# First layer's small heads: parts in half of the array's rows, groups in alternating halves, scores and turned scores issued in turn

## What is computed

```python
xn = _layernorm(x, axis=-1)
q, k, v = split(xn @ qkv_w + qkv_b)          # 16 heads of 8 features
a = softmax(q @ k.T * scale, axis=-1) @ v    # per head, no mask in this layer
x = x + (a @ proj_w + proj_b) + moe(xn)
```

## Time and profile before

| | |
|---|---|
| median of three runs | 2050.64 us (2049.12 to 2058.69) |
| the profiled execution | 2065.7 us, of which 2063.9 us from first to last instruction |
| mean granted clock of PE in it | 0.95 |
| first layer's heads in it | from 102.5 us; last new head's scores at 340.9 us |
| PE busy over the span | 1846.2 us (89%) |
| DVE, ACT, POOL busy | 1512.0 (73%), 973.7 (47%), 900.6 (44%) us |

### The profile page before, as it was taken

The page is one execution under the profiler, slowest core; times in us unless marked ns, Lnnn a source line. Parts: engine busy times, 40 slices in busy tenths (PEclk is TensorE's granted clock), DMA queues, the critical chain, the costliest instruction groups (busy, mean ns, idle before and its releaser), DMA issues. The chain is left out here.

```text
span 2063.9 us, 33097 instructions
## 1 busy us (share of the span) xinstructions
PE 1846.2 (89%) x9971; PEld 1013.2 (49%) x9971; DVE 1512.0 (73%) x4413; ACT 973.7 (47%) x2251; POOL 900.6 (44%) x1307
## 2 busy tenths in 40 slices
PE   6399998578998994899799999989999999999998
PEld 3233333345555662334466666744445555555543
DVE  6477776476664765899577677657877787888898
ACT  3167676246664442622377777733333333333332
POOL 1566661045552330112066677745544455433341
PEclk9789999579999995999899999999999999999999
DMA  8552222363232006990465446411131443524211
GB/s 283 140 117 36 29 29 51 49 245 81 38 75 39 23 22 123 159 196 24 120 195 154 147 142 185 132 50 45 44 107 56 127 119 88 137 71 109 61 32 31
DMA packets 240309, 201.81 MB, mean 98 GB/s; under 512 B 26853, under 2 KB 222731, under 8 KB 239498
## 3 DMA queue, kind: packets, MB, share of 16 engines
q1 hardware_dynamic: 222042, 171.29, 33.1%
q0 software_dynamic: 17376, 28.29, 5.5%
q10 hardware_dynamic: 720, 0.11, 0.0%
HBM read 116.74 MB, written 82.89 MB: 97 GB/s over the span
## 5 line engine op out<-in xcount | busy, mean ns | idle before, releaser
L2845 DVE SCALAR_TENSOR_TENSOR x<-f_m,f_gs,x 128x128 f32<-128x128 f32 x1024 | 353.4, 348 | 81.7 <-PE f_m L2670 54.7
L512 DVE TENSOR_REDUCE a_nmax<-a_s 128x1 f32<-128x512 f32 (+3 forms) x512 | 278.9, 585 | 125.6 <-PE a_s L323 51.9
L2218 POOL TENSOR_SCALAR a_lg<-a_lg,a_rinv 128x256 f32<-128x256 f32 (+1 forms) x256 | 226.4, 902 | 150.4 <-DVE a_rinv L2255 149.9
L2670 PE MATMUL f_m<-f_wo,f_oT 128*128 128x512 f32 x512 | 261.4, 595 | 1.7 <-DVE x L2845 1.0
L428 ACT ACTIVATE a_pT<-a_st 128x512 f32<-128x512 f32 (+3 forms) x512 | 228.8, 519 | 35.1 <-PE a_st L349 12.5
L2618 POOL DMA_INDIRECT f_yg<-yslot,slot x160 | 152.1, 950 | 202.0 <-PE f_s L2704 96.8
L323 PE MATMUL a_s<-t_kp,t_qp 96*128 96x512 bf16 (+3 forms) x512 | 165.9, 359 | 11.4 <-DVEq L496 7.6
L346 PE MATMUL a_st<-t_qp,t_kp 99*128 99x512 bf16 (+3 forms) x512 | 162.8, 353 | 1.7 <-ACT a_pT L428 1.2
L2798 ACT COPY f_pT<-f_t 128x512 f32<-128x512 f32 x128 | 75.2, 588 | 147.1 <-PE f_t L2712 111.0
L2845 DVE SCALAR_TENSOR_TENSOR f_val<-f_m,gate,f_val 128x128 f32<-128x128 f32 x336 | 113.5, 344 | 41.8 <-PE f_m L2670 27.8
L2670 PEld LDWEIGHTS f_m<-f_wo,f_oT 128*128 128x128 f32 x512 | 91.3, 190 | 97.5 <-issue 82.0
(11 more groups left out here) (436 smaller groups left out, 3823.7 us busy)
## 6 DMA issues: line engine op xcount, KB each, us to landing
a_band<-band SPq DMA_DIRECT2D x64, 512.0 KB, 4.6
band<-s_hole SPq DMA_DIRECT2D x16, 1032.0 KB
band<-a_rows SPq DMA_DIRECT2D x64, 256.0 KB, 4.1
yslot<-f_ys SPq DMA_DIRECT2D x45, 256.0 KB
f_xs<-spare_rows SPq DMA_DIRECT2D x9, 832.0 KB
w_gate_up<-f_wgu_in SPq DMA_DIRECT2D x4, 1536.0 KB, 17.2
t_qp<-parts SPq DMA_DIRECT2D x192, 32.0 KB
t_kp<-parts SPq DMA_DIRECT2D x192, 32.0 KB
```

What stands on the lines that cost most here:

```text
L512: v.tensor_reduce(nmax[:, h % 4, qt:qt + 1], s_ps[(b * H * QT + u) % R][:, 0:n], AX.X, ALU.max, negate=True)\
L2218: last = pool.tensor_scalar(lg[:, g % 2, half, p, c0:c0 + n], lg[:, g % 2, half, p, c0:c0 + n], rinv[:, g % 2, p, qt:qt + 1], None, ALU.mult)
L2670: pe.matmul(ps[:, :], left, w, start=True, stop=True).then_inc(full, 1)
L2845: ins = v.scalar_tensor_tensor(out, ps[:, e * P:(e + 1) * P], gate, out, ALU.mult, ALU.add)
```

## The change

Only the first layer is touched (`causal` false).

- `half_of(h)` gives a head a row base of 0 (groups 0 and 2) or 64 (groups 1 and 3) and one of eight column blocks. `load_half` puts the 48 part rows at base + 0 to 31 and base + 35 to 50; the three rows between, base + 32 to 34, are the maxima's.
- Scores and turned scores both read the same 51 rows from the base, where they read 96 and 99. Since the scores now read the maxima's rows too, these must be zero in `qp` when the scores are made. For sequences 1 to 3 SP issues a DMA of three rows of zeros ahead of each group's 12 loads, 12 such DMAs in all, and PE's wait counts it.
- `maxima` writes rows m to m + 2 of its bank, m = 32 or 96, and ACT copies from and to these.
- POOL sets a second block of ones, of 3 x 2048 words.
- PE's order: score tile n of head h and turned tile n of head h - 3 in turn, `values` after the second pair, `maxima` after the third.

```diff
+def half_of(h):
+    return 64 * (h // 4 % 2), h // 8 * 4 + h % 4
+def load_half(sp, k, parts, c, b, g, sem):
+    i, j = PAIRS[c]
+    base, col = half_of(4 * g)
+    first = base + (8 * c if c < 4 else 8 * c + 3)
+    for dst, s, part in ((k.qp, 0, i), (k.kp, 1, j)):
+        sp.dma_start(dst[first:first + 8, col:col + 4, :], parts[s, part, 32 * g:32 * g + 32, bass.ds(b * T, T)]
+                     .rearrange("(h r) t -> r h t", r=8)).then_inc(sem, 16)
...
+                        sp.dma_start(qp[m:m + 3, col:col + 4, :], qp[0:3, 8:12, :]).then_inc(heads_in[g], 16)
...
-                    last = pe.matmul(ps[:, 0:n], qp[0:MR, h, qt * P:(qt + 1) * P], kp[0:MR, h, 0:n],
+                    r = slice(base, base + (MR if causal else 51))
+                    last = pe.matmul(ps[:, 0:n], qp[r, col, qt * P:(qt + 1) * P], kp[r, col, 0:n],
...
-                        last = pe.matmul(out[:, q0:T], kp[0:KT, i % H, kt * P:(kt + 1) * P], qp[0:KT, i % H, q0:T],
+                        r = slice(base, base + (KT if causal else 51))
+                        last = pe.matmul(out[:, q0:T], kp[r, col, kt * P:(kt + 1) * P], qp[r, col, q0:T],
...
+                    for n in range(QT):
+                        if new:
+                            scores(n)
+                        if live(h - 3):
+                            turned_scores(h - 3, (n,))
+                        if n == 1 and live(h - 7):
+                            values(h - 7)
+                        if n == 2 and live(h - 1):
+                            maxima(h - 1)
...
-                    act.copy(qp[MR:MR + 3, i % H, :], m_ps[MR:MR + 3, :]).then_inc(mt_read, 1)
+                    act.copy(qp[m:m + 3, col, :], m_ps[m:m + 3, :]).then_inc(mt_read, 1)
...
+            pool.memset(k.kp[32:35, 0:8, :].bitcast(F32), TWO_ONES).then_inc(filled, 1)
```

More of the change, by code:

```diff
@@ L220, in small_heads, with home @@
     R = 3
+    def home(h):
+        if causal:
+            return 0, MR, h
+        base, col = half_of(h)
+        return base, base + 32, col
     with ExitStack() as ctx:
@@ L269, in _ @@
                 for c in range(len(PAIRS)):
-                    load_pair(sp, k, parts, ROWS, c, 0, g, heads_in[g])
+                    if causal:
+                        load_pair(sp, k, parts, ROWS, c, 0, g, heads_in[g])
+                    else:
+                        load_half(sp, k, parts, c, 0, g, heads_in[g])
                 if g == 1 and not causal:
@@ L286, in _ @@
                     sp.wait_ge(st_done, (b - 1) * QT * H + QT * (4 * g + 4))
-                    for c in range(len(PAIRS)):
-                        load_pair(sp, k, parts, ROWS, c, b, g, heads_in[g])
+                    if causal:
+                        for c in range(len(PAIRS)):
+                            load_pair(sp, k, parts, ROWS, c, b, g, heads_in[g])
+                    else:
+                        _, m, col = home(4 * g)
+                        sp.dma_start(qp[m:m + 3, col:col + 4, :], qp[0:3, 8:12, :]).then_inc(heads_in[g], 16)
+                        for c in range(len(PAIRS)):
+                            load_half(sp, k, parts, c, b, g, heads_in[g])
             if causal:
@@ L318, in scores @@
                     if qt == 0 and h % 4 == 0:
-                        pe.wait_ge(heads_in[h // 4], (b + 1) * LOADS)
+                        pe.wait_ge(heads_in[h // 4], (b + 1) * LOADS + (0 if causal else 16 * b))
                     pe.wait_ge(max_done, b * H * QT + u + 1)
@@ L322, in scores @@
                     ps = s_ps[(b * H * QT + u) % R]
-                    last = pe.matmul(ps[:, 0:n], qp[0:MR, h, qt * P:(qt + 1) * P], kp[0:MR, h, 0:n],
+                    base, _, col = home(h)
+                    r = slice(base, base + (MR if causal else 51))
+                    last = pe.matmul(ps[:, 0:n], qp[r, col, qt * P:(qt + 1) * P], kp[r, col, 0:n],
                                      start=True, stop=not causal)
@@ L332, in maxima @@
                     misc_free(b, h, False)
+                    _, m, _ = home(i % H)
                     for qt in range(QT):
-                        last = pe.matmul(m_ps[MR:MR + 3, qt * P:(qt + 1) * P], m3[:, i % 2, qt, :], k.ident_bf[:, :],
+                        last = pe.matmul(m_ps[m:m + 3, qt * P:(qt + 1) * P], m3[:, i % 2, qt, :], k.ident_bf[:, :],
                                          start=True, stop=True)
@@ L345, in turned_scores @@
                         out = st_ps[w % R]
-                        last = pe.matmul(out[:, q0:T], kp[0:KT, i % H, kt * P:(kt + 1) * P], qp[0:KT, i % H, q0:T],
+                        base, _, col = home(i % H)
+                        r = slice(base, base + (KT if causal else 51))
+                        last = pe.matmul(out[:, q0:T], kp[r, col, kt * P:(kt + 1) * P], qp[r, col, q0:T],
                                          start=True, stop=not causal)
@@ L374, in step @@
                 new = live(0)
[L375 to L391, removed]
+                if causal:
+                    if new:
+                        scores(0)
+                        scores(1)
+                    if live(h - 3):
+                        turned_scores(h - 3, (0,))
+                    if new:
+                        scores(2)
+                    if live(h - 3):
+                        turned_scores(h - 3, (1,))
+                    if new:
+                        scores(3)
+                    if live(h - 7):
+                        values(h - 7)
+                    if live(h - 1):
+                        maxima(h - 1)
+                    if live(h - 3):
+                        turned_scores(h - 3, (2, 3))
+                else:
+                    for n in range(QT):
+                        if new:
+                            scores(n)
+                        if live(h - 3):
+                            turned_scores(h - 3, (n,))
+                        if n == 1 and live(h - 7):
+                            values(h - 7)
+                        if n == 2 and live(h - 1):
+                            maxima(h - 1)
                 if h % 4 == 0 and live(h - 12):
@@ L434, in step @@
                     act.wait_ge(mt_full, b * H + i + 1)
-                    act.copy(qp[MR:MR + 3, i % H, :], m_ps[MR:MR + 3, :]).then_inc(mt_read, 1)
+                    _, m, col = home(i % H)
+                    act.copy(qp[m:m + 3, col, :], m_ps[m:m + 3, :]).then_inc(mt_read, 1)
                 if live(h - 3):
@@ L803, in _ @@
             for c in range(len(PAIRS)):
-                load_pair(sp, k, parts, 8, c, 0, 0, k.heads_in[0])
+                load_half(sp, k, parts, c, 0, 0, k.heads_in[0])
             for q in range(Q):
@@ L820, in _ @@
             pool.memset(k.kp[MR:MR + 3, :, :].bitcast(F32), TWO_ONES).then_inc(filled, 1)
-            pool.wait_ge(filled, 3)
+            pool.memset(k.kp[32:35, 0:8, :].bitcast(F32), TWO_ONES).then_inc(filled, 1)
+            pool.wait_ge(filled, 4)
         @block.tensor
```

## The result

The changed kernel takes 2112.84 us (median of four runs, 2106.27 to 2118.07), the kernel before 2049.88 us beside it: 1.029 times the time before, 95% interval 1.027 to 1.031. Slower by 63 us, as forecast (2106). In the profiled execution (2106.27 us) the first layer's heads, from the first score tile (101.6 us) to the last (390.6), take 289 us where they took 239 (102.5 to 341.4). The next stage begins at 423.8 us, not 375.3. The instructions behind it are the same and take 1680.6 us, not 1688.6, in the two profiled executions. Of the changed kernel that execution is the shortest of four, of the kernel before it is a long one (2065.7 us): so the two profiles lie 41 us apart and the medians 63. What follows says which of the two a number comes from.

A forecast was written before the change was run, and what follows sets the result against it. Waits bound a step, with PE and ACT in balance through ACT's copy of the maxima. Half the groups at a low clock give +58 - 2.4, about +55 us: 2121 against the profile, 2106 against the median; range 2057 to 2145.

The forecast's parts named there:

- The bound: First layer's heads: no engine full (PE 91%), waits set a step; taking time off PE alone gives nothing.
- The chain at the full clock: First layer's steps through ACT's copy of the maxima: phase 2 takes 3.32 us, a group 15.9; +13 us in all.
- values of phase 3: In phase 3's step, values wait for DVE's row maxima and output copy, starting at 2.85 us.
- phase 1: This step of a group, where the maxima wait for DVE's division: 3.30 us at the full clock, was 3.52.
- The gain at the start: Three first steps without values, at the low clock, fall from 4.04 us to about 3.2: -2.4 us.
- The clock: First layer's heads: granted clock falls repeatedly, half the groups at 21.8 us, half at 15.9: +58 us; chance 0.60.
- Phases 3 and 0 together: These two steps of a group at the low clock: 6.6 us for phase 3 and 6.0 for phase 0.
- Hidden work: POOL's new memset, SP's 12 extra DMAs at 0.30 us each and the loads cost nothing: all zero.
- the clock stays up: Rival: clock stays at full level in the first layer's heads; +13 us, 2064 us; chance 0.22.
- the clock stays down throughout: Rival: clock stays low through the whole first-layer heads' stage; +100 us, 2150 us; chance 0.10.
- the rival without side-by-side halves: Rival: pairs cost 0.43 us, falling into PE's wait; only a few us on top of the forecast; no chance given.

The follow-up runs named there:

- layout alone: The changed kernel with the old issue order on PE (51 rows, groups in alternating halves): 0.999 of the kernel before.
- pairs first: All pairs, then values, then maxima, ACT's copy behind all four exponentials; changed kernel with 51 or 64 rows, kernel before with 96: 0.996, 0.997, 0.997 of the kernel before.
- the output's copy: The kernel before with DVE's copy of the finished group's output ahead of phase 3's first two row maxima, in both layers: 0.992 of the kernel before, 2040.0 us.
- filled run: The changed kernel with three unused 128-row matmuls in PE's wait ahead of the second turned tile, in phases 2, 3 and 0: 1.011 of the kernel before.
- one half: The changed kernel with all heads at row 0, so no two matmuls run side by side: 1.084 of the kernel before, 2244 us.
- order alone: The kernel before with only PE's new issue order, 96 and 99 rows, no halves: 1.011 of the kernel before, 2093.87 us.

## Why the prediction was right, and where not

**The bound.** Right. The layout alone took PE's busy share from 91% to 82% and gained nothing (0.999); both moves that helped, pairs first and the output's copy, shortened a wait.

**The chain at the full clock.** Right to a few hundredths: 3.31 us from maxima to maxima (3.32 predicted), values of phase 3 at 2.82 us (2.85), phase 1, from 359.86 to 363.14, 3.28 (3.30). Added up, a group's steps take 15.9 us (values to values 3.52, 3.52, 4.20 and 4.69), as predicted. Filling the waits holds the clock at 0.99 and gives 1.011 of the time before, 23 us, of which some 5 are the fillers' own. That leaves 18 for the chain, where 13 were predicted. The gain at the start, put at 2.4 us, accounts for part of it: from the first score tile to the first values it is 24.2 us before and in the filled run, and 22.7 in the changed kernel.

**The clock.** The size was right, and it is the largest term: half of 14 groups at 5.9 us more is 41 us, and the filled run gives 37 of 63 by the medians and 25 of 50 in the profiled heads. The place was right too: it falls around phase 3, ahead of whose values PE has only thin matmuls and the maxima for the longest time. How the 41 us came about was not, and there luck helped. I took half of the groups as low throughout, at 21.8 us each. In fact eleven of 14 fell and none stayed low: the longest has 20.2 us (values of phase 3 to the next, 160.81 to 180.97). More groups, each for less, come to nearly the same, 42% of the time. Phases 3 and 0 together took 12.79 us against 12.6, though the first began at the full clock. The reason was right only as a product: I read it as a matter of thin matmuls in a longer stretch without values, and then, for the layout alone, expected the rows to be enough. They are not (clock 1.00), nor is the order (0.97).

**Hidden work.** Right: no wait of PE for a load of `t_qp` shows in this stage. POOL's memset takes 1.80 us ahead of 7.91 us of idle time. The 12 DMAs take 0.68 us of SP's queue each, not 0.30, and nothing waits for them.

**The rivals.** That the clock stays up did not happen (0.79). The Trainium skill (TensorE: Matmul & The Clock Gate, Part 1) says that the gate goes by how busy PE has been; this case's traces do not agree, since in one half PE was busy 96% of 390 us and stayed at 1.2 GHz. That the clock stays down throughout did not happen to the changed kernel but to that one. The price that was mis-sized is that of the rival without side-by-side halves, "only a few us". At the full clock it stands: order alone, with serial pairs of 96 and 99 rows, has 16.3 us a group against 15.9, 5 us over 14 groups. But I left out that serial thin matmuls do not let the clock come back. One half's heads took 412.6 us against the changed kernel's 289.0, and its time is 176 us above the kernel before on its chip.

What stays open: what exactly the chip counts. The runs show that rows act on the clock, and that the layout and the order act together; that the order acts by the spacing of the full matmuls is inferred, and the runs give no law.

## What to carry to other kernels

Before cutting PE's time, look for a chain as long as the step that runs through another engine; here 1.68 us of a phase-2 step of 3.15 lay in ACT's copy and exponential, and taking nine points off PE's busy share was worth nothing. Matmuls through few rows are not only no faster one by one, they can cost the clock when the order changes with them (0.79 here, 1.00 with the old order), so read the granted clock of the stage after any such change. And ask of each engine's order which item somebody waits for: one copy moved ahead of two row maxima gave 0.8%, where the new layout in its best order gave 0.4%. The intervals overlap, and the copy was moved in both layers; in the first layer's heads alone the two are about even (228.4 us against 231.6 and 228.6).

## What the runs showed of the hardware

- Matmuls of 51 rows in the two halves of the array start within 0.01 us of each other and take the time of one, also when both have 128 columns of weights.
- A change between full and column-tiled matmuls costs PE 0.10 us whichever side comes first; the 51-row ones behave the same (values to third pair 1.00 us against 0.90 to the maxima).
- In phase 3 of the changed kernel a score tile in one half starts 0.40 us ahead of a turned tile in the other half that is issued before it (335.21 and 335.61); the same shows at other phases 3 (164.15 and 164.55).
- 13 more rows of zeros raised the mean granted clock of the stage from 0.82 to 0.90; serial 51-row matmuls, busy 96%, left it at 0.50 for 390 us, where the same order with 96 and 99 rows had 0.97.
- Adding three full matmuls to three steps in four took 1.8% of the time off (1.029 to 1.011 of the kernel before, each on its own chip).
